# Layer 0's attention by query chunks of 512 for four heads at once, with outputs and sums in 32-column tiles of TensorE

## The reference, cut to what matters

```python
q = (h @ Wq.T).reshape(B, S, 16, 64).transpose(0, 2, 1, 3)
k = (h @ Wk.T).reshape(B, S, 4, 64).transpose(0, 2, 1, 3)
v = (h @ Wv.T).reshape(B, S, 4, 64).transpose(0, 2, 1, 3)
k, v = jnp.repeat(k, 4, axis=1), jnp.repeat(v, 4, axis=1)
scores = jnp.einsum('bhqd,bhkd->bhqk', q, k) * 64 ** -0.5
scores = scores + causal[None, None]
probs = jax.nn.softmax(scores, axis=-1)
out = jnp.einsum('bhqk,bhkd->bhqd', probs, v)
return out.transpose(0, 2, 1, 3).reshape(B, S, 1024) @ Wo.T
```

## Time and profile before

| | us |
|---|---|
| median of 3 runs (1603.08 to 1613.52) | 1605.54 |
| the profiled execution | 1614.19 |
| its span in the profile | 1612.5 |
| PE busy in it | 1317.3 |
| DVE busy | 1052.0 |
| ACT busy | 654.1 |
| POOL busy | 200.5 |

### The profile page before, as it was taken

One profiled execution on the slowest core, in us unless ns is written; L12 is line 12 of the kernel. 1 busy time (PEld: TensorE's weight loads), 2 busy tenths in 40 slices (PEclk: granted clock), 3 DMA queues, 4 the chain that ended last, 5 costly groups with the idle time before them and its releaser, 6 DMA issues. The chain is left out here.

```text
span 1612.5 us, 19740 instructions
## 1 busy us (share of the span) xinstructions
PE 1317.3 (82%) x6220; PEld 802.8 (50%) x6220; DVE 1052.0 (65%) x1626; ACT 654.1 (41%) x1176; POOL 200.5 (12%) x413
## 2 busy tenths in 40 slices
PE   3689999999999999427999967415898988559996
PEld 3345555555555555225777745312343443146874
DVE  4656556475746552376999986745677875058996
ACT  1133433334343433014555534221366666225663
POOL 0001111111111112001111100111011111001110
PEclk9679999999999999758999989755699999569997
DMA  2110202112020201106766610043032211102210
GB/s 84 32 35 1 58 10 53 36 26 48 13 62 0 61 4 27 30 10 139 151 138 144 148 34 1 1 128 81 2 71 58 48 45 33 46 23 97 107 63 27
DMA packets 42784, 87.67 MB, mean 54 GB/s; under 512 B 13552, under 2 KB 31608, under 8 KB 37496
## 3 DMA queue, kind: packets, MB, share of 16 engines
q1 hardware_dynamic: 42720, 86.86, 22.5%
HBM read 69.47 MB, written 8.45 MB: 48 GB/s over the span
## 5 line engine op out<-in xcount | busy, mean ns | idle before, releaser
L586 ACT ACTIVATE shared<-ps 128x1024 f32<-128x1024 f32 (+7 forms) x256 | 165.8, 650 | 358.8 <-PE ps L433 358.2
L448 PE MATMUL ps<-shared,Vg 128*65 128x512 f32 (+3 forms) x768 | 291.0, 487 | 10.8 <-POOL shared L617 8.5
L1226 PE MATMUL ps<-qA 128*128 128x512 f32 x960 | 255.2, 402 | 17.8 <-DVE qA L1338 12.8
L499 DVE TENSOR_REDUCE mraw<-ps 128x1 f32<-128x512 f32 (+3 forms) x304 | 195.9, 659 | 89.4 <-PE ps L400 61.4
L904 DVE TENSOR_REDUCE mraw<-ps 128x2 f32<-128x1024 f32 (+3 forms) x160 | 174.0, 1114 | 83.7 <-PE ps L824 61.0
L1226 PEld LDWEIGHTS ps<-qA 128*128 128x128 f32 x960 | 178.8, 191 | 75.3 <-DVE shared L1351 17.5
L948 ACT ACTIVATE shared<-ps 128x512 f32<-128x512 f32 (+2 forms) x320 | 154.2, 563 | 131.7 <-PE ps L840 131.3
L431 PE MATMUL ps<-qA,kH 128*128 128x512 f32 (+3 forms) x384 | 168.3, 446 | 2.6 <-DMA qB<-mT 2.6
L394 PE MATMUL ps<-kH,qA 128*128 128x512 f32 (+3 forms) x384 | 162.6, 463 | 6.3 <-DVE mraw L499 2.8
L448 PEld LDWEIGHTS ps<-shared,Vg 128*65 128x65 f32 x768 | 98.4, 138 | 118.2 <-issue 83.4
L1280 ACT CAST qA<-shared 128x512 fp32r<-128x512 f32 x160 | 99.4, 621 | 135.3 <-DVE shared L1358 134.7
(11 more groups left out here) (250 smaller groups left out, 1571.2 us busy)
## 6 DMA issues: line engine op xcount, KB each, us to landing
shared<-comb SPq DMA_DIRECT2D x96, 256.0 KB, 4.4
qB<-qA SPq DMA_DIRECT2D x8, 1024.0 KB, 7.0
rB<-a0rec_dram SPq DMA_DIRECT2D x8, 1024.0 KB, 7.2
shared<-comb SPq DMA_DIRECT2D x8, 1024.0 KB, 4.4
q_split<-qA SPq DMA_DIRECT2D x8, 512.0 KB
qA<-q_split SPq DMA_DIRECT2D x16, 256.0 KB, 4.4
rB<-a1rec_dram SPq DMA_DIRECT2D x32, 128.0 KB, 2.8
e0wUp<-in_w SPq DMA_DIRECT2D x48, 64.0 KB, 4.6
```

The source lines that it names most:

```text
L448: ins = nc.tensor.matmul(O[0:65, lo:hi], k.Vg[par][:, kt, :], k.PT[:, slot % PTR, lo:hi], start=(kt == 0), stop=(kt == 4 * ch + 3))
L499: ins = nc.vector.tensor_reduce(out, bank[:, 0:n_h * width].rearrange("p (h w) -> p h w", w=width), AX, ALU.max)
L586: nc.scalar.activation(k.PT[:, slot % PTR, kt * P:S], score_banks(slot)[:, kt * P:S], ACT.Exp, scale=scale).then_inc(p_full, 1)
L1226: ins = nc.tensor.matmul(bank[0:M, :], w[par][:, at:at + M], h[:, cols], start=(r == 0), stop=(r == 2))
```

## The change

The attention of a group is written by units instead of slots. A unit is a query chunk of 512 and a key tile, for all four heads: 4 units for the first chunk, 8 for the second, 12 in a group, 96 in all. The order of a unit n on TensorE is: score products of unit n, with preparation jobs in between (`parts`), and then the values of unit n - 2.

- Scores use three single banks in turn (2 to 4), one exponential for each bank (narrow units put two or four heads in a bank). Probabilities of three units are kept (`k.P64`).
- Values: for each head, two products of 32 columns of V, at partitions 0, 32, 64 and 96 of two banks (O), and for the sums four products with a 32-column tile of ones (`k.ones32`) into a third bank (SUMS). `Vg` and its copies on GpSimd go.
- A finished chunk is copied out by ScalarE (one bank) and VectorE (one bank and the sums). Sums are gathered, inverted, stored and spread for each chunk, and one multiplication of 128x1024 normalises four heads of a chunk. One output projection follows for each chunk.
- Preparation is per chunk as well: three projections, the maxima of the chunk's queries (11 or 27 products), one transpose. Ahead of the first unit only the first chunk of group 0 is prepared; its second chunk is dealt over units 0 to 3, group 1 over units 4 to 10, and each later group over 11 units of the group before it, in proportion to the units' widths.
- Nothing is in a hardware loop any longer: all eight groups are written out.

```diff
--- before
+++ after
-    def plan(prep, fin):
-
-        order = []
-        if prep:
-            order += [(2 + i // 2, "proj", i) for i in range(NPROJ)]
-            order += [(6 + i * 20 // NMAX, "max", i) for i in range(NMAX)]
-            order += [(26, "turn", i) for i in range(2)]
-        if fin:
-            order += [(FIN_SLOT + i, "fin", i) for i in range(NFIN)]
...
-        def score_banks(slot):
-            first = 2 + 2 * (slot % 2)
-            return k.ps[:, first * 512:(first + 2) * 512]
...
-            def values(g, par, slot):
-                h, kt = divmod(slot, TPB)
-                if slot == 0:
-                    pe.wait_ge(v_done, g + 1)
-                pe.wait_ge(p_full, NSLOT * g + slot + 3)
-                for ch in range(CPB - 1, kt // 4 - 1, -1):
-                    if ch == kt // 4:
-                        pe.wait_ge(masked, NSLOT * g + slot + 1)
-                    if kt == 0:
-                        pe.wait_ge(oU_full, CPB * (REP * g + h) + ch + 1)
-                    lo, hi = max(ch * 512, kt * P), (ch + 1) * 512
-                    ins = nc.tensor.matmul(O[0:65, lo:hi], k.Vg[par][:, kt, :], k.PT[:, slot % PTR, lo:hi],
-                                           start=(kt == 0), stop=(kt == 4 * ch + 3))
-                ins.then_inc(pt_free, 1)
...
-            def copy_out(g, h, ch):
-                dve.wait_ge(pt_free, TPB * (REP * g + h) + 4 * (ch + 1) + PTR)
-                dve.wait_ge(on_done, REP * g + h + 1)
-                cols = slice(ch * 512, (ch + 1) * 512)
-                nc.vector.tensor_copy(k.oU[0:65, h, cols], O[0:65, cols]).then_inc(oU_full, 1)
...
-            def normalise(g, h):
-
-                if h == 0:
-                    dve.wait_ge(rec_ld, 16 * g)
-                o = k.oN[(h % 2) * hd:(h % 2 + 1) * hd, h // 2, :]
-                nc.vector.tensor_tensor(o, k.oU[0:hd, h, :], k.rB[0:hd, h * S:(h + 1) * S], ALU.mult)\
-                    .then_inc(on_done, 1)
...
+    CT = P // REP
+    UNITS = [(0, kt) for kt in range(4)] + [(1, kt) for kt in range(TPB)]
+    NU = len(UNITS)
+    STEPS = NU * G
+    RING = 3
+    LAG = 2
+    SCORE_BANKS = 3
+    U = 1 + REP // 2
...
+    def score_jobs(n):
+
+        size = max(1, 512 // (512 - unit_lo(n)) // 2 * 2) if 512 - unit_lo(n) <= 256 else 1
+        return [tuple(range(h, h + size)) for h in range(0, REP, size)]
...
+    def jobs_of(g, qc):
+
+        return [("proj", g, qc, u) for u in range(U)] + [("max", g, qc, j) for j in range(len(MAXES[qc]))] + \
+            [("turn", g, qc, 0)]
+
+    def spread_over(jobs, first, last):
+
+        widths = [512 - unit_lo(n) for n in range(first, last)]
+        total = sum(widths)
+        at, upto = first, widths[0]
+        for j, job in enumerate(jobs):
+            while (j + 0.5) / len(jobs) * total > upto:
+                at += 1
+                upto += widths[at - first]
+            plan.setdefault(at, []).append(job)
+
+    plan = {-1: jobs_of(0, 0)}
+    spread_over(jobs_of(0, 1), 0, 4)
+    spread_over(jobs_of(1, 0) + jobs_of(1, 1), 4, NU - 1)
+    for g in range(2, G):
+        spread_over(jobs_of(g, 0) + jobs_of(g, 1), NU * (g - 1), NU * g - 1)
+    for g in range(G):
+        plan.setdefault(NU * g + 10, []).append(("fin", g, 0, 0))
+        plan.setdefault(NU * (g + 1) + 6, []).append(("fin", g, 1, 0))
...
+    def parts(n):
+
+        heads = score_jobs(n) if n < STEPS else [()]
+        fills = due.get(n, [])
+        size = -(-len(fills) // len(heads))
+        return [(hs, fills[size * i:size * (i + 1)]) for i, hs in enumerate(heads)]
...
+        O = [k.bank(5), k.bank(6)]
+        SUMS = k.bank(7)
...
+                    elif kind == "max":
+                        if j == 0:
+                            pe.wait_ge(w_free, index["proj", g, qc, U - 1] + 1)
...
+                def values(n):
+
+                    g, (qc, kt) = n // NU, UNITS[n % NU]
+                    kv, b = divmod(g, B)
+                    if on_diagonal(n):
+                        pe.wait_ge(masked, diagonals[n + 1])
+                    else:
+                        pe.wait_ge(p_done, first_score[n + 1])
+                    if kt == 0 and n:
+                        pe.wait_ge(o_act, 2 * g + qc)
+                        pe.wait_ge(o_dve, 2 * g + qc)
+                    lo = unit_lo(n)
+                    first, last = kt == 0, closes(n)
+                    for p in range(2):
+                        for i in range(2):
+                            for half in range(2):
+                                at = 2 * i + half
+                                v = k.V[:, b * TPB + kt, kv * hd + half * CT:kv * hd + (half + 1) * CT]
+                                nc.tensor.matmul(O[p][CT * at:CT * (at + 1), lo:512], v,
+                                                 probs(n)[:, 2 * p + i, lo:512], start=first, stop=last,
+                                                 skip_group_check=True)
+                    for h in range(REP):
+                        ins = nc.tensor.matmul(SUMS[CT * h:CT * (h + 1), lo:512], k.ones32[:, :],
+                                               probs(n)[:, h, lo:512], start=first, stop=last, skip_group_check=True)
+                    ins.then_inc(pv_done, 1)
...
+                for n in range(STEPS + LAG):
+                    for at, (hs, fills) in enumerate(parts(n)):
+                        if hs:
+                            scores(n, first_score[n] + at, hs)
+                        for idx in fills:
+                            job(idx)
+                    if n >= LAG:
+                        values(n - LAG)
+                job(index["fin", G - 1, 1, 0])
...
+                def copy_out(n):
+
+                    g, (qc, kt) = n // NU, UNITS[n % NU]
+                    cols = slice(qc * 512, (qc + 1) * 512)
+                    dve.wait_ge(pv_done, n + 1)
+                    if g:
+                        dve.wait_ge(on_done, 2 * g + qc - 1)
+                    nc.vector.tensor_copy(k.S64[:, :], SUMS)
+                    nc.vector.tensor_copy(k.oU64[:, 1, cols], O[1]).then_inc(o_dve, 1)
+
+                def recips(g, qc):
+
+                    sm, rs = sums_at(qc)
+                    dve.wait_ge(sum_ld[qc], 16 * REP * (g + 1))
+                    nc.vector.reciprocal(rs, sm).then_inc(rec_done, 1)
+
+                def normalise(g, qc):
+
+                    cols = slice(qc * 512, (qc + 1) * 512)
+                    dve.wait_ge(rec_ld[qc], 16 * REP * (g + 1))
+                    dve.wait_ge(o_act, 2 * g + qc + 1)
+                    nc.vector.tensor_tensor(k.oN64[:, :, cols], k.oU64[:, :, cols], k.rB64[:, :, cols], ALU.mult)\
+                        .then_inc(on_done, 1)
...
+                for n in range(STEPS + LAG):
+                    if n > LAG and closes(n - LAG - 1):
+                        copy_out(n - LAG - 1)
+                    at = n % NU
+                    if at in (3, 5) and n >= NU:
+                        (recips if at == 3 else normalise)(n // NU - 1, 1)
+                    if at in (7, 9):
+                        (recips if at == 7 else normalise)(n // NU, 0)
+                    for idx in due.get(n, []):
+                        take(idx)
...
+                    if n > LAG and closes(n - LAG - 1):
+                        copy_out(n - LAG - 1)
+                    if n >= RING and n < STEPS:
+                        act.wait_ge(pv_done, n - RING + 1)
+                    for at, (hs, fills) in enumerate(parts(n)):
+                        if hs:
+                            lo = unit_lo(n)
+                            s = first_score[n] + at
+                            act.wait_ge(s_full, s + 1)
+                            src = score_bank(s)[:, 0:len(hs) * (512 - lo)].rearrange("p (a q) -> p a q", a=len(hs))
+                            nc.scalar.activation(probs(n)[:, hs[0]:hs[-1] + 1, lo:512], src, ACT.Exp, scale=scale)\
+                                .then_inc(p_done, 1)
+                        for idx in fills:
+                            if JOBS[idx][0] == "proj":
+                                high(idx)
+                copy_out(STEPS - 1)
...
+                        tile = probs(n)[:, :, lo:lo + P]
+                        nc.gpsimd.affine_select(tile, tile, [[0, REP], [1, P]], ALU.is_ge, 0.0, base=0,
+                                                channel_multiplier=-1).then_inc(masked, 1)
...
+                def gather_sums(g, qc):
+
+                    sp.wait_ge(o_dve, 2 * g + qc + 1)
+                    for h in range(REP):
+                        sp.dma_start(sums_at(qc)[0][CT * h:CT * (h + 1), :],
+                                     k.S64[CT * h:CT * h + 1, :]
+                                     .rearrange("o (p j) -> o p j", p=CT)).then_inc(sum_ld[qc], 16)
+
+                def spread(g, qc):
+
+                    cols = slice(qc * 512, (qc + 1) * 512)
+                    sp.wait_ge(rec_done, 2 * g + qc + 1)
```

(72 more changed lines are left out.)

483 lines of the change are left out of this document (211 added, 272 removed).

## The result

The changed kernel takes 1640.02 us, median of 4 runs (1631.74 to 1644.27), against 1609.52 us for the kernel before (4 runs, 1603.08 to 1613.52): ratio 1.019, 95% interval 1.013 to 1.025. It is 30 us slower. The forecast was 1620 us (range 1583 to 1665), 14 us slower, called "same", near its upper edge.

What follows compares the result with a forecast made beforehand. TensorE, in program order, was taken to bound the attention stage. Six groups +21, group 7 -6, start +6 and end -7 gave +14 us, on the median of 1605.5 us 1620 us, range 1583 to 1665.

Steps and rivals of the forecast that it cites:

- the walk: Unit-by-unit timing of the changed attention stage, with TensorE's waits for banks and other engines: 76.0 us a group for 72.5.
- The values' stream: TensorE's values products in the changed attention: 27.1 us a group instead of 30.9, 2.9 a unit at 512 columns.
- The stream as a whole: All TensorE work of an attention group without stalls: 63.5 us after the change, 67.4 before.
- The stalls: TensorE's waits in a changed group, for banks, subtractions, transposes and copies: 12.5 us in sum.
- Six groups: +21 us: Groups 1 to 6 of the attention stage: 76.0 us each for 72.5, 21 us more in all.
- rival 2: In the changed stage the granted clock falls to an average of 0.9, costing 47 us: 1667 us; chance 0.15.
- The start: Up to group 1: first score at 69 us, unit 4 near 108, group 1 at 172; +6 us, bounds +1 and +12.
- Group 7 and the end: Last group, without jobs, -6 us; from last values to last addition, 17 us for 24, -7 us.
- Rival 1: Bursts of preparation jobs stall TensorE only half as much, 6 us less in seven groups: 1578 us; chance 0.15.
- rival 3: Instruction starts bound TensorE in the values' 32-column products, 9.5 us a group, 76 in all: 1696 us; chance 0.08.
- "Same": Total time within about 1% (16 us) of the kernel before: chance 0.42, against faster 0.18 and slower 0.40.

Runs made afterwards that it cites:

- e4: The changed kernel with the products for the sums left out except at each chunk's first key tile, so sums are incomplete: 1589.0 us in one run.
- e7: The changed kernel with preparation jobs reordered, three PSUM banks for jobs and two for scores: 1571.8 us, ratio 0.974 to the kernel before.
- e1: The changed kernel with three unused fp32 matmuls of 512 columns put in the gap of each group's first unit: 1630.1 us in one run.
- e2: The changed kernel with a group's first three projections alone in its first unit, the other 43 jobs dealt over the next ten: 1635.0 us in one run.
- e5: The changed kernel with both chunks of group 0 prepared ahead of its first unit: 1646.5 us in one run.
- e3: The changed kernel with three PSUM banks for preparation jobs instead of two, and two for scores instead of three: 1612.0 us in one run.
- e6: The changed kernel with projections, maxima and transposes dealt in another order, still on two job banks: 1616.7 us in one run.
- e8: e7 with a finished chunk's outputs copied by ScalarE alone, VectorE copying only the sums: 1571.0 us, ratio 0.973 to the kernel before.

## Why the prediction was right or wrong

The time lies within the range, and of the mechanism the waits and the values were right; the clock was not in the sum. Unit by unit, the walk ahead of the run against group 3 of the changed kernel (us; starts of L461, and TensorE's idle times over 0.15 us, which the profile counts from modelled ends):

| unit | 0 | 1 | 2 | 3 | 4 | 5 | 6 | 7 | 8 | 9 | 10 | 11 |
|---|---|---|---|---|---|---|---|---|---|---|---|---|
| stall forecast | 3.4 | 0.1 | 0.85 | 0 | 1.6 | 2.2 | 1.75 | 0.75 | 0.53 | 0.1 | 1.26 | 0 |
| idle measured | 2.78 | 0 | 0 | 0 | 1.08 | 0.97 | 0.41 | 0 | 0 | 0 | 0.79 | 0 |
| measured length | 13.16 | 3.65 | 5.16 | 3.46 | 8.07 | 6.49 | 9.17 | 6.74 | 6.42 | 5.58 | 7.45 | 3.12 |

The eleven units other than the first add up to 65.3 us. With the 10.47 us that the first took in group 1, at full clock, that is 75.8, for a forecast group of 76.0. How near that is, is partly luck, as the next points show.

- **The values' stream** (27.1 for 30.9 us a group) was right: 2.72 us a unit at 512 columns before the switch into the tiles, and e4 prices a group's ten sets at 6.2 us for 6.5.
- **The stream as a whole** (63.5 us) was too short by about 3 us. Group 7 has no jobs and idles 0.3 of its 51.5 us, so its stream is 51.2 us for the 48.0 walked; a group of e7 idles 1.3 of 68.0, which leaves 66.7. Where the 3 us go was not traced.
- **The stalls** were right in place and cause, and too large in sum: a group at full clock less the 66.7 of e7 leaves 9.1 us for 12.5. So the two errors cancel. Idle time in the rows: 2.78 us behind the third projection (forecast 3.1), 1.08 at a transpose, 0.73 and 0.41 at a third maximum; in units 2, 7 and 8, where 2.1 us were walked, none shows:

```profile
355.14 0.27 PE L435 MATMUL ps<-ident,mmax 128*16 128x128 f32 x1 [1.08 <-DVE mmax L535]
...
363.95 1.09 PE L423 MATMUL ps<-kH,qA 128*128 128x512 f32 x2 [0.73 <-DVE mraw L531]
...
369.65 1.10 PE L423 MATMUL ps<-kH,qA 128*128 128x512 f32 x3 [0.41 <-DVE mraw L531]
```

- **"Six groups: +21 us"** is the term that was mis-sized: 31.8. Group 1, which kept its clock, took 75.8 us; group 2 77.4 and groups 3 to 6 78.5. The excess of these five over 75.8 is 12.4 us, and e1 shows it to be the clock's answer to the first unit's gap; without it the term would have been +19. The sum had that gap at its bare length, with nothing for the clock. The clock stood as rival 2, at a chance of 0.15 and as an alternative to the forecast. The two were not alternatives: the gap that the forecast itself put at 3 us came ahead of the fall in five groups of six. The granted clock of a group came out at 0.96, just past the 0.97 named, and the period at 78.5, between the 76 of the forecast and the 80 named for rival 2, at a quarter of the price given (47 us), since each dip was over after 3 to 7 us.
- **The start** was +9.4 for +6, within its bounds. The +6 itself compares the 172 us of a first score product with an exponential of the kernel before, at 166.3; from its first score product, at 165.0, the same walk gives +7. The parts (69 us, unit 4 at 106) were right, and units 4 to 11 took 68 us for 64. Their two chains of projections are the same kind of gap; how much of the 4 us is clock was not tried.
- **Group 7 and the end** were -5.5 and -6.3 for -6 and -7. Group 7 took 51.5 us for the 48.9 walked, but the 54.8 of the kernel before, from first to last exponential, are 57.0 between the ends used here, so the difference held by luck.
- Rival 1 (the bursts don't bite) and rival 3 (starts bound TensorE) are refuted by the period of 75.8 us at full clock and by e4.
- "Same" was given 0.42 and "slower" 0.40. Measured is 1.9% more, interval 1.3 to 2.5%, beyond the 1% that the forecast took for no change. With 31.8 in place of 21 the sum is +25 us, for a measured +30.

## What to carry to other kernels

Between two jobs that share few banks, and of which the second needs what other engines make of the first, the in-order queue of TensorE needs other work at least as long as the whole chain of cast, subtraction and semaphore. Deal jobs by that distance, not by an even share of time. Here an idle gap of 2.8 us on a busy TensorE cost nearly twice its length in most groups, and one of 1.9 us nearly that in a third of them, so price such gaps with the clock, and look for them first when a kernel has less to do and takes longer. A large rewrite that moves the time little can hide a better stream under worse waits: here the same products in another order, with three banks for jobs instead of two, are 2.6% faster than the kernel before.

## What the runs showed of the hardware

- The clock in groups 1 to 6, by TensorE's longest idle time in a group: behind gaps of 2.78 us it fell in 23 of 24 groups (changed kernel, e2, e4, e5), behind 3.13 us in five of six (e3), behind 1.93 us in two of six (e6). Where the longest was 1.15 us (e7, e8) it stayed at 2.4 GHz in all twelve groups. It also fell twice with nothing over 1.1 us in the ten us before, once in e1 and once in e5, so no single length of gap divides the cases. A dip lasted 3 to 7 us, during which a 512-column matmul of 0.39 us took 0.63.
- 32-column products cost per set of four what their passes cost, from 0.85 us at 512 columns to 0.22 at 128 (e4), and the 48 loads and matmuls of a unit's values in 2.7 us were no limit.
